# Inverse square roots moved to POOL as powers, and reciprocal row sums turned by transposes

## The reference

```python
def _layernorm(x, axis=-1, eps=1e-05):
    m = jnp.mean(x, axis=axis, keepdims=True)
    v = jnp.var(x, axis=axis, keepdims=True)
    return (x - m) / jnp.sqrt(v + eps)
...
scores = jnp.einsum('bhqd,bhkd->bhqk', qh, kh) / math.sqrt(d_k)
scores = jnp.where(mask == 0, jnp.float32(-jnp.inf), scores)
...
# softmax over the 375 keys, times v, heads joined, output projection
```

## Time and profile before

| | us |
|---|---|
| median of 3 runs | 2579.9 |
| lowest and highest run | 2578.73, 2580.28 |
| the profiled execution's own time | 2579.06 |
| its span, first to last instruction | 2577.3 |
| TensorE busy | 2280.6 (88%) |
| VectorE busy | 1291.3 (50%) |
| ScalarE busy | 1047.2 (41%) |
| POOL busy | 258.4 (10%) |

### The profile page before, as it was taken

How to read it: one execution, slowest core, us unless ns; L and a number is a source line. 1 busy time by engine, 2 the same in 40 slices (tenths; PEclk the granted TensorE clock), 3 DMA queues, 4 the chain that set the end, 5 groups by cost and what they waited for, 6 DMA issues and landing times.

```text
span 2577.3 us, 45875 instructions
## 1 busy us (share of the span) xinstructions
PE 2280.6 (88%) x15822; PEld 1761.7 (68%) x15822; DVE 1291.3 (50%) x3990; ACT 1047.2 (41%) x2806; POOL 258.4 (10%) x297
## 2 busy tenths in 40 slices
PE   4999996999967599949999999999959939999988
PEld 3788874777745467637777787877647727888855
DVE  5888873222245522264454444545542257777723
ACT  2777771222122112214444444444402217878811
POOL 0000000111141034200000000000014400000010
PEclk8999997999988689969999999999969969999999
DMA  6888855222245212310000000000042158888600
GB/s 190 207 200 202 198 135 232 83 82 82 70 138 162 113 46 63 92 45 13 7 17 11 13 11 11 13 11 11 5 183 64 56 157 203 204 202 200 153 11 22
DMA packets 149438, 252.60 MB, mean 98 GB/s; under 512 B 14736, under 2 KB 124640, under 8 KB 146544
## 3 DMA queue, kind: packets, MB, share of 16 engines
q1 hardware_dynamic: 138560, 220.31, 31.7%
q0 software_dynamic: 10656, 29.37, 3.6%
HBM read 191.04 MB, written 58.59 MB: 97 GB/s over the span
## 4 chain that ended last, share of the span: by engine, by line
PE 77%; DVE 12%; DMA 4%; issue 4%; ACT 2%; SPq 2%; DVEq 0%; ACTq 0%; POOLq 0%
PE bank L1635 8%; PE bank L924 8%; PE bank L955 6%; PE bank L1665 6%; PE bank L838 5%; PE bank L834 5%; PE bank L1690 5%; PE bank L912 4%; PE bank L869 4%; PE bank L825 3%; PE bank L1678 3%; PE bank L849 3%; PE bank L907 3%; PE bank L1942 2%; PE bank L1928 2%
## 5 line engine op out<-in xcount | busy, mean ns | idle before, releaser
L924 PE MATMUL bank<-ident,arena 112*125 112x112 f32 x2352 | 372.9, 276 | 3.4 <-DVE arena L1185 0.3
L924 PEld LDWEIGHTS bank<-ident,arena 112*125 112x125 f32 x2352 | 337.5, 188 | 49.2 <-issue 12.6
L1212 ACT ACTIVATE arena<-arena,mx 112x375 f32<-112x375 f32 x512 | 308.6, 604 | 111.2 <-DVE mx L1164 109.7
L1164 DVE CUSTOM_DVE_ANT_0 arena<-bank,maskf 112x375 f32<-112x375 f32 x512 | 274.1, 541 | 81.2 <-PE bank L907 79.7
L907 PE MATMUL bank<-kS,qS 128*112 128x376 f32 x512 | 236.3, 462 | 42.7 <-DMA kS<-key_halves 23.4
L1176 DVE TENSOR_REDUCE mx<-bank 112x1 f32<-112x375 f32 x256 | 128.6, 543 | 246.8 <-PE bank L912 246.4
L1635 PE MATMUL bank<-arena 128*128 x532 | 231.8, 559 | 3.2 <-ACT arena L1739 3.2
L1185 DVE COPY arena<-bank 125x336 f32<-125x336 f32 x448 | 214.1, 502 | 32.4 <-PE bank L924 32.4
L1212 ACT ACTIVATE arena<-bank,mx 112x375 f32<-112x375 f32 x272 | 156.0, 575 | 178.9 <-DVE mx L1176 150.9
L955 PE MATMUL bank<-arena 125*32 125x112 f32 (+1 forms) x4608 | 202.0, 264 | 2.9 <-DVE arena L1185 2.9
L955 PEld LDWEIGHTS bank<-arena 125*32 125x32 f32 (+1 forms) x4608 | 143.7, 118 | 85.6 <-issue 67.9
(11 more groups left out here) (246 smaller groups left out, 3666.5 us busy)
## 6 DMA issues: line engine op xcount, KB each, us to landing
kS<-key_halves SPq DMA_DIRECT2D x256, 188.0 KB, 5.5
qS<-query_halves SPq DMA_DIRECT2D x128, 224.0 KB, 4.6
arena<-in_ctxT SPq DMA_DIRECT2D x64, 376.0 KB, 4.8
key_halves<-arena SPq DMA_DIRECT2D x64, 376.0 KB, 5.9
arena<-in_f_out SPq DMA_DIRECT2D x21, 768.0 KB, 4.5
query_halves<-arena SPq DMA_DIRECT2D x32, 448.0 KB, 4.2
arena<-in_f_up SPq DMA_DIRECT2D x4, 2816.0 KB, 19.1
arena<-results SPq DMA_DIRECT2D x20, 448.0 KB, 7.5
```

Source lines behind the costliest of these rows:

```text
L924: m = pe.transpose(bank[2 + g % 2][0:KT, k * S:(k + 1) * S], pr[:, g % t.NR, k * KT:(k + 1) * KT], ident[0:S, 0:S])
L1164: dve.tensor_tensor_reduce(sm[:, g % 2, :], bank[g % 2][0:S, 0:SK], maskf[:, :], 1.0, 3e38, ALU.add, ALU.min, mx[:, g % t.NR:g % t.NR + 1])\
L1212: act.activation(pr[:, g % t.NR, :], src, ACT.Exp, bias=mx[:, g % t.NR:g % t.NR + 1], scale=-1.0, accum_out=row_sum(t, b)[:, h:h + 1]).the ...
```

## The change

1. The steps of the second norm become five (`LN_STEPS` from 15 to 4): mean and variance twice, epsilon, the product for the mean, the rows. The inverse root is taken by POOL, as a power with the exponent -0.5 held in a small tile `root`; a new semaphore, `rooted`, tells VectorE. `store_tokens` and `add_b2` call it for each pair, and `last_roots` for each chunk of the last norm. As the list of steps is shorter, n and r take earlier slots.
2. Kind i becomes a transpose. Layers 0 and 3 transpose the same tile, 2 transposes in place of 2 products. In layer 2 VectorE first spreads the 16 reciprocals over the 112 x 1024 tile `on`, and TensorE transposes it in 2 groups of 4, in place of 2 groups of 8 products. Layer 2 counts two steps of the chain semaphore for each sample in place of one.
3. One more constant is set by POOL at the start, and the counts that wait for constants grow by one.

```diff
-LN_STEPS = 15
+LN_STEPS = 4
...
-        self.NC = 2 if self.masked else 1
+        self.NC = 2 if self.H == 16 else 1
...
-                        m = pe.matmul(dst[:, j * S:(j + 1) * S], heads16[:, j * P:(j + 1) * P], ident[0:S, 0:S],
-                                      start=True, stop=True)
+                        m = pe.transpose(dst[:, j * S:(j + 1) * S], heads16[:, j * P:(j + 1) * P], ident[0:S, 0:S])
...
                     for j in range(4):
-                        for e in range(2):
-                            h = 2 * (o + j) + e
-                            m = pe.matmul(dst[e * dh:(e + 1) * dh, j * S:(j + 1) * S],
-                                          rinv[:, b % 2, h:h + 1].broadcast_to([S, dh]), ident[0:S, 0:S],
-                                          start=(j == 0), stop=(j == 3), skip_group_check=True)
+                        m = pe.transpose(dst[:, j * S:(j + 1) * S], on[:, (o + j) * P:(o + j + 1) * P], ident[0:S, 0:S])
...
-                elif i == 3:
-                    ins = dve.tensor_scalar(half, u, -0.5, None, ALU.mult)
-                elif i == 4:
-                    ins = dve.tensor_scalar(y.bitcast(I32), u.bitcast(I32), -0.5, float(0x5f3759df), ALU.mult, ALU.add)
-                elif i < 14 and i % 3 == 2:
-                    ins = dve.tensor_tensor(a, y, y, ALU.mult)
-                elif i < 14 and i % 3 == 0:
-                    ins = dve.tensor_tensor(a, a, half, ALU.mult)
-                elif i < 14:
-                    ins = dve.scalar_tensor_tensor(out=y, in0=a, scalar=1.5, in1=y, op0=ALU.add, op1=ALU.mult)
-                elif i == 14:
+                elif i == 3:
+                    dve.wait_ge(rooted, L * (B // 2) + pair + 1)
                     ins = dve.scalar_tensor_tensor(out=nmr[:, two], in0=mv[:, two, 0], scalar=-1.0, in1=y,
                                                    op0=ALU.mult, op1=ALU.mult)
...
+                    else:
+                        dve.wait_ge(t.chain, c0 + 1)
+                        dve.tensor_copy(on[:, :].rearrange("p (h d) -> p h d", d=dh),
+                                        rinv[:, p, :].unsqueeze(2).broadcast_to([S, 16, dh])).then_inc(t.chain, 1)
...
+        def reciprocal_root(pool, t, pair):
+
+            at = ln.at(2 * t.L + 1)
+            two = slice(2 * pair, 2 * pair + 2)
+            pool.wait_ge(ln.dve, at + t.row_steps[("ln", pair, 2)])
+            pool.tensor_tensor(rstd[:, two], newton[:, :], root[:, 0:2], ALU.pow).then_inc(rooted, 1)
...
+        def last_roots(pool):
+
+            for c in range(NCH):
+                four = slice(c * CHUNK, (c + 1) * CHUNK)
+                pool.wait_ge(normed, (c + 1) * (2 * CHUNK + 1))
+                pool.tensor_tensor(rstd[:, four], t1[0][:, four], root[:, :], ALU.pow).then_inc(rooted, 1)
```

More of the change, by code:

```diff
@@ L477, in build @@
         epsc = sb("epsc", [P, 1])
+        root = sb("root", [S, CHUNK])
         def part(at, n, rows=P):
@@ L530, in build @@
         lgt = sb("lgt", [S, B * E])
-        newton = sb("newton", [S, 2, 4])
+        newton = sb("newton", [S, 2])
         gather_id = sb("gather_id", [P, max(BLOCKS)], U32)
@@ L592, in build @@
         b2_added = sem("b2_added")
+        rooted = sem("roots_by_pool")
         padded = sem("values_padded")
@@ L1105, in row_norm @@
                 two = slice(2 * pair, 2 * pair + 2)
-                var, u, y, a = mv[:, two, 1], newton[:, :, 0], rstd[:, two], newton[:, :, 2]
-                half = newton[:, :, 1]
+                u, y = newton[:, :], rstd[:, two]
                 before = [("stats", 2 * pair), ("stats", 2 * pair + 1)] + \
@@ L1114, in row_norm @@
                 elif i == 2:
[L1115 removed]
+                    ins = dve.tensor_scalar(u, mv[:, two, 1], EPS, None, ALU.add)
                 elif i == 3:
[L1117 to L1126 removed]
+                    dve.wait_ge(rooted, L * (B // 2) + pair + 1)
                     ins = dve.scalar_tensor_tensor(out=nmr[:, two], in0=mv[:, two, 0], scalar=-1.0, in1=y,
@@ L1308, in stack_sync @@
                     context(sp, t, b + 2)
+        def reciprocal_root(pool, t, pair):
[3 more added lines that the diff above has]
+            pool.tensor_tensor(rstd[:, two], newton[:, :], root[:, 0:2], ALU.pow).then_inc(rooted, 1)
         def store_tokens(pool, t, f):
             for pair in range(B // 2):
+                reciprocal_root(pool, t, pair)
                 pool.wait_ge(ln.xn, (2 * t.L + 1) * (B // 2) + pair + 1)
@@ L1977, in last_norm @@
             four = slice(c * CHUNK, (c + 1) * CHUNK)
-            u, half, a = (t1[k][:, four] for k in range(3))
-            y = rstd[:, four]
-            done = c * (2 * CHUNK + LN_STEPS - 3)
+            u = t1[0][:, four]
+            done = c * (2 * CHUNK + 1)
             for b in range(c * CHUNK, (c + 1) * CHUNK):
@@ L1988, in last_norm @@
             done += 2 * CHUNK
[L1989 to L1992, removed]
-                elif i == 3:
-                    ins = dve.tensor_scalar(half, u, -0.5, None, ALU.mult)
-                elif i == 4:
-                    ins = dve.tensor_scalar(y.bitcast(I32), u.bitcast(I32), -0.5, float(0x5f3759df), ALU.mult, ALU.add)
-                elif i % 3 == 2:
-                    ins = dve.tensor_tensor(a, y, y, ALU.mult)
-                elif i % 3 == 0:
-                    ins = dve.tensor_tensor(a, a, half, ALU.mult)
-                else:
-                    ins = dve.scalar_tensor_tensor(out=y, in0=a, scalar=1.5, in1=y, op0=ALU.add, op1=ALU.mult)
-                ins.then_inc(normed, 1)
-                done += 1
+            dve.wait_ge(normed, done)
+            dve.tensor_scalar(u, mv[:, four, 1], EPS, None, ALU.add).then_inc(normed, 1)
+            done += 1
             if c == 0:
@@ L2009, in last_norm @@
                                          op0=ALU.subtract, op1=ALU.mult).then_inc(centred, 1)
-            dve.wait_ge(normed, done)
+            dve.wait_ge(rooted, 4 * (B // 2) + c + 1)
             dve.wait_ge(beta_added, min(B // 2, (c + 1) * CHUNK // 2))
@@ L2092, in _ @@
             nc.gpsimd.memset(ones[:, :], 1.0).then_inc(consts, 1)
+            nc.gpsimd.memset(root[:, :], -0.5).then_inc(consts, 1)
             nc.gpsimd.memset(tri[:, :], 1.0).then_inc(consts, 1)
@@ L2095, in _ @@
                 .then_inc(consts, 1)
-            pool.wait_ge(consts, 9)
+            pool.wait_ge(consts, 10)
             nc.gpsimd.tensor_copy(lane[:, :], lanei[:, :]).then_inc(consts, 1)
@@ L2108, in _ @@
                                     base=0, pattern=[[-16, 8]], channel_multiplier=1).then_inc(consts, 1)
-            pool.wait_ge(consts, 17)
+            pool.wait_ge(consts, 18)
             nc.gpsimd.affine_select(out=sel16[:, :], in_=sel16[:, :], compare_op=ALU.is_ge, fill=0.0,
@@ L2123, in _ @@
                     add_beta(pool)
+                    last_roots(pool)
         @block.tensor
         def _(pe):
-            pe.wait_ge(consts, 18)
+            pe.wait_ge(consts, 19)
             for L in range(4):
@@ L2138, in _ @@
         def _(act):
-            act.wait_ge(consts, 18)
+            act.wait_ge(consts, 19)
             for L in range(4):
@@ L2150, in _ @@
         def _(dve):
-            dve.wait_ge(consts, 18)
+            dve.wait_ge(consts, 19)
             dve.tensor_reduce(sel2[:, :], sel16[:, :].rearrange("p (j e) -> p e j", e=2), AX_X, ALU.add)\
                 .then_inc(consts, 1)
-            dve.wait_ge(consts, 19)
+            dve.wait_ge(consts, 20)
             dve.wait_ge(loaded["x"], 16)
```

## The result

The changed kernel takes **2561.2 us** (median of 4 runs, 2560.35 to 2562.28) against 2579.4 of the kernel before beside it: ratio 0.9927, interval 0.9915 to 0.994, 18 us faster. The prediction was 2564.4, faster.

The account below looks back on a forecast made before the run. TensorE carries most of the chain, so VectorE's time counts only where TensorE stands still for it. Terms -8.2, -4.1, -2.2, -9.0, -2.8, +9.2, +2.4 sum to -14.7 us; 2579.1 - 14.7 = 2564.4 us; range 2552 to 2577.

Parts of the forecast that it names:

- Layer 1's norms: Layer 1's pair norms: the power shortens TensorE's wait for the rows by 1.37 us in six pairs, -8.2 us.
- Stage ends: Ends of attention in layers 0, 2 and 3: the last pair's norm saves 1.37 us three times, -4.1 us.
- Last norm: Last chunk's final norm: one of twelve steps is left before the centring, which hides the power, -2.2 us.
- Layer 2's transposes: Layer 2's reciprocals: transposes for products gain 0.56 us per sample after a 0.33 us late start, 16 samples, -9.0 us.
- Rival 2: Layer 2's copy runs at one element per cycle or is held up: 8.6 us longer, 2573; chance 0.12.
- Layers 0 and 3, transposes at nothing: Layers 0 and 3: some 0.25 us per sample leave TensorE, but its stall for VectorE's minimum grows by that; nothing.
- Newton's steps gone: Layers 0 and 3: without Newton's steps between the minima, -0.20 us per pair, 7 pairs in 2 layers, -2.8 us.
- The moved steps: Earlier slots: rows waited for in layers 0 and 3, +9.2 us; second query product waits in layer 2, +2.4 us.
- 1 (a slow power): POOL's power is slow and its wait replaces Newton's chain: slower than before, 2602 at p = 3; chance 0.13.
- 3 (the moved steps cost nothing): Layers 0, 2 and 3: the slots around the moved steps give way, 11.6 us less, 2553; chance 0.12.
- 4 (layer 1 gives back half): Layer 1: another wait, a score or a context, shows where the rows were waited for, 2568; chance 0.08.
- 5: Layer 0: the first power costs a program load once, 2565 to 2567, or 2570 by the skill's figure; chance 0.05.

Follow-up runs that it names:

- power twice: The changed kernel with each power of the attention norms done twice, first into a scratch tile; ratio 0.9982 to the kernel before.
- transposes only: The kernel before with only the transposes and the copy added, Newton's steps and old places kept; ratio 0.9964 to the kernel before.
- slow copy: The changed kernel with layer 2's copy written as a maximum of the tile with itself, two sources; ratio 0.9979 to the kernel before.
- products kept: The changed kernel with the transposes of layers 0 and 3 turned back into products, layer 2's kept; ratio 0.9940 to the kernel before.
- old slots: The changed kernel with eleven empty places, so row transposes and router's products stand where they stood before; ratio 0.9904 to the kernel before.
- one slot and halves: The changed kernel with one empty place before the transposes of the rows and layer 2's copy in halves; ratio 0.9900 to the kernel before.
- copy in halves: The changed kernel with layer 2's copy in two halves of 512 elements; ratio 0.9950 to the kernel before.

## Why the prediction was right, by its own steps

**Layer 1's norms, -8.2.** The mechanism is shown. p came out at 0.91 us where 0.8 was taken: POOL's operation is 0.71 instead of 0.5, the two hand-overs are 0.2 together instead of 0.3. Four pairs gained 1.29 each (1.37 forecast); the power done twice gives 0.67 per pair back. In the tail the last two pairs gained 5.8 together, not 2.7, and that is not the power's. There TensorE's granted clock falls from 2.4 to 1.2 GHz as the attention runs out. Windows by stretch (TensorE's granted clock is the third number from the end), pair by pair: the kernel before, after, and the power twice:

```profile
849.00:860.00 11.00, 7.71 (x47) 7.16 (x47) 5.17 (x24) 1.71 (x4) 0.66 (x1) 0.84 0.07 21
860.00:871.00 11.00, 6.19 (x23) 4.80 (x24) 5.19 (x24) 0.54 (x1) 0.96 (x2) 0.51 0.07 22
```

```profile
846.00:855.00 9.00, 6.08 (x47) 5.64 (x47) 4.17 (x16) 1.71 (x4) 1.41 (x2) 1.00 0.10 27
855.00:864.00 9.00, 5.17 (x24) 3.58 (x24) 3.48 (x14) 0.65 (x2) 2.10 (x3) 0.63 0.09 25
```

```profile
852.00:861.00 9.00, 7.73 (x47) 6.99 (x47) 2.47 (x10) 1.71 (x4) 1.71 (x3) 0.81 0.09 27
861.00:873.00 12.00, 6.38 (x24) 4.90 (x24) 4.31 (x16) 0.55 (x1) 3.01 (x5) 0.58 0.06 19
```

The same 47 matmuls take 7.71 us at 0.84 and 6.08 at 1.00. The short wait doesn't ensure this, though. Of the eleven traces with it (two are of the changed kernel) seven keep the clock (tail 15.7 to 16.8 us) and four lose it (18.3 to 18.7, the same code in layer 1). The experts behind the tail take 256.0 to 256.2 us or 258.1 to 258.5, always the shorter where the tail was long, so that the two together are 272.9 to 274.7 in all eleven. Counted so, the last two pairs gave 5.2, of which 2.6 are the power's by the four pairs in front, and the other 2.6 go with the clock. The three kernels with a longer wait (before, transposes only, power twice) all lose the clock there; three against four of eleven is a hint, no proof, that the wait decides it.

**Stage ends, -4.1.** Right. The stretches gave 1.6 and 0.9 in layers 0 and 3, but they hold the clock too, which fell at different moments. TensorE's wait for the rows doesn't: it is 4.63 us at all three ends before and 3.33, 3.32 and 3.30 after, -3.9 in all. The power twice makes it 4.01, 4.00 and 3.97. Layer 2's, before and after:

```profile
1876.99 0.57 PE L876 MATMUL bank<-ident,xn 112*128 112x112 f32 x4 [4.63 <-DVE xn L1135]
```

```profile
1863.42 0.57 PE L873 MATMUL bank<-ident,xn 112*128 112x112 f32 x4 [3.32 <-DVE xn L1122]
```

**Last norm, -2.2.** Right up to the last products: they start 1.66 us after epsilon, right behind the centring, and POOL's 1.18 us lie under it. But 1.0 of the 2.2 us is lost again behind them, and that the prediction had at nothing. At the end of the program each engine has a closing instruction, DRAIN. POOL's ends 5.9 us after the end of POOL's last operation, in all 14 traces. Before, that operation was an addition of beta that ended at 2471.81, a hundred us early. Now it is the last power, which ends at 2554.11, so that POOL's DRAIN lasts until 2560.01, while SyncE is done with the output at 2558.9; the span ends at 2560.24. The closing instructions of POOL and SyncE (count, duration in ns three times, start), before and after:

```profile
L451 POOLq DRAIN  x1: 15518/15518/15518, 2462.2 to 2462.2; - x1
L451 SPq DRAIN  x1: 7/7/7, 2577.1 to 2577.1; - x1
```

```profile
L451 POOLq DRAIN  x1: 7108/7108/7108, 2552.9 to 2552.9; - x1
L451 SPq DRAIN  x1: 7/7/7, 2559.0 to 2559.0; - x1
```

From the last products to the end it is 5.89 us in every kernel with the power and 4.84 in the two without. What one would gain by taking the last chunk's root elsewhere wasn't tried.

**Layer 2's transposes, -9.0.** -9.4 without the powers, 751.21 - 742.04 = -9.2 with them. Copy, hand-over, late start: each as forecast. Rival 2 would have been 8.6 longer; the slow copy shows nearly that, 0.51 x 16 = 8.2. The Trainium skill, "VectorE: DVE Perf Modes", "Mode 2×_2P — use both read ports for one tensor", puts a one-source copy in SBUF at two elements per cycle; the trace agrees, also for a source with step 0: 0.694 us against 1.225 with two sources.

**Layers 0 and 3, transposes at nothing.** Right, 0.2 us (products kept) to 0.4 (transposes only).

**Newton's steps gone, -2.8.** With the old slots the streams of layers 0 and 3 are 1.15 and 1.24 below the kernel before: -2.4, in which the transposes' 0.1 and 0.4 are contained.

**The moved steps, +9.2 and +2.4.** The sum is right by luck (11.6 forecast, 10.8 measured); its parts are not. In layer 0 TensorE waits for the rows 0.81 us in each of 7 pairs, in layer 3 0.59 (there VectorE waits for the root, 3.1 us in all, but had been early), by the waits of TensorE in the two streams:

```profile
PE bank L873 <- DVE xn L1122: 5.7, 7, 0.8
...
PE bank L873 <- DVE arena L1122: 4.1, 7, 0.6
```

3.7 and 3.1 us come off with the old slots: 0.49 per pair, not 0.66. In layer 2 it is 4.0, not 2.4. From sample to sample it is 0.55 us for each of six pairs, not 0.40, and 0.6 more in the last window, which the prediction didn't count. The second query product does wait, but 0.17 us by its record; what the rest is stays open.

**Rivals.** 1 (a slow power) falls with 0.71 us. 2 falls. 3 (the moved steps cost nothing) falls: with the old slots the streams are 10.8 us shorter. 4 (layer 1 gives back half) falls. 5 falls: the first power took 0.73 us and began 0.08 after the end of the step before it (108.60), so no load is seen. The Trainium skill, "GPSIMD Engine Reference", "Instruction dispatch", has approximately 6 us for the first call to a freshly loaded kernel; this trace doesn't show them at the first power.

**The sum.** The terms come to, measured: -7.7 (six pairs without the clock), -3.9, -2.2, -9.3, 0, -2.4, +6.8, +4.0: -14.7, as forecast, with errors of 2.4 and 1.6 us in the moved steps that nearly cancel. Three things stand beside it that the prediction didn't have: +1.0 for POOL's DRAIN, +2.3 in the experts of layer 0, where the clock rises later (below), and -2.6 with the clock of layer 1's tail. With them it is -14.0. The spans of the two traces of the changed kernel lie 17.1 and 13.2 below that of the kernel before; the 3 us on one side and the 1 on the other lie in the start, the head of layer 1 and experts 2, which move from trace to trace. So the mechanism was right in its large terms, and that the total came out within 3 us owes something to luck: of what was missed, two costs and a gain nearly cancel too. Which of the two timings, 18 or 14 us, is nearer to the kernel's own mean can't be said from these runs.

## What to carry to other kernels

A chain of small dependent steps on one engine is worth its length wherever the next engine stands for it, and nothing elsewhere: one power on an idle engine, 0.9 us with both hand-overs, replaced eleven links of 0.20. When steps are taken out of a hand-made order, all behind them moves up; look where the consumer lands against its producer. Here one empty place gave 12.9 us in three streams, nearly as much as the norms' shortening (7.7 + 3.9 + 2.2). An engine that has been idle is not free at the very end of a program: ask when its last operation now ends. Compare stretches of the trace, not totals, when stretches that no edit touches move by 2 us; and see whether such a stretch moves in every kernel with the change before calling it chance.

## What the hardware showed that was not expected

A power of -0.5 on POOL takes 0.71 us for 112 x 2 elements and 1.18 for 112 x 4; by these two sizes that is an estimate of 0.23 us per column above 0.24.

POOL's closing DRAIN ends 5.9 us after its last operation (2477.70 after 2471.81 before, 2560.01 after 2554.11 in the changed kernel). It costs time only where that operation is late.

TensorE's granted clock changes between 1.2 and 2.4 GHz at moments that differ by some 4 us from kernel to kernel, and each costs or gives 2 to 4 us in stretches that are the same code. Part of this follows the kernel and not chance. In the experts of layer 0 the clock is at 1.2 GHz, and 28 to 32 us after the last pair's transposes it is rising in the kernel before and with transposes only (mean 0.74 and 0.80), and still at 0.50 in all twelve traces with the power; in the next 4 us it rises there too (0.51 to 0.71). It is the first block of the experts against the second, 2.3 us for the stretch. Why isn't shown; the code in between is the same. Transposes only, then the changed kernel:

```profile
419.00:423.00 4.00, 3.02 (x14) 2.14 (x12) 0.39 (x1) 0.36 (x1) 1.80 (x2) 0.96 0.99 371
```

```profile
421.00:425.00 4.00, 3.06 (x9) 1.97 (x8) 0.39 (x1) 0.36 (x1) 1.95 (x3) 0.50 0.91 367
425.00:429.00 4.00, 3.13 (x11) 2.49 (x10) 0.39 (x1) 0.36 (x1) 0.00 (x0) 0.73 0.93 302
```

At the end of layer 2 sixteen matmuls took 3.68 us in the changed kernel and 6.58 in the one with one slot and halves, whose clock was 0.52 there (timelines of both, then the stretch of the latter):

```profile
1856.42 3.68 PE L866 MATMUL bank<-arena,oT 128*112 128x256 f32 x16 [1.53 <-DVE oT L1046]
```

```profile
1841.90 6.58 PE L866 MATMUL bank<-arena,oT 128*112 128x256 f32 x16 [1.39 <-DVE oT L1046]
```

```profile
1842.00:1848.00 6.00, 6.00 (x15) 4.46 (x16) 0.00 (x0) 0.00 (x0) 0.00 (x0) 0.52 0.00 0
```

This fall of the clock ahead of the last waits stands in all three kernels whose copy was altered (slow copy, copy in halves, one slot with halves: 2.1 to 3.6 us) and in none of the other eleven traces, so it too seems to belong to the kernel; how the copy could bring it about isn't shown. What differs between two executions of one kernel is seen in experts 2: the clock of the changed kernel rose there between 44 and 48 us after the last pair's transposes in the first trace (0.86) and not before 48 in the second (0.50), 2.1 us for the stretch.
